# Householder tridiagonalisation on one NeuronCore: reciprocal of the divisor kept as the gain, a second ScalarE product, the minus-M form of the update, sign counts in blocks of eight, and the layers' loop written out

## The reference

```python
L_norm = d_inv_sqrt[:, None] * L * d_inv_sqrt[None, :]
_, U = jnp.linalg.eigh(L_norm)
agg = jnp.einsum('mn,bnd->bmd', U.T, features)
h = jax.nn.relu(agg @ W1 + b1)
out = h @ W2 + b2
return jnp.einsum('nm,bmd->bnd', U, out)
```

## Time and profile before

| | before |
|---|---|
| median of 3 runs | 1329.01 us |
| profiled execution | 1329.98 us, its span 1328.2 us |
| reflections, first to last tail written (L418) | 11.1 to 392.2 us |
| end of `spectral_basis` on VectorE (L441) | 402.67 us |
| start of the layers' first matmul | 523.44 us |
| VectorE, GpSimd busy in 0 to 403 us | 336.26, 286.13 us |
| granted TensorE clock in 0 to 403, 403 to 523, 523 to 1328 us | 1.00, 0.70, 0.94 |

### The profile page before, as it was taken

How to read it: one execution, slowest core, us unless ns; L and a number is a source line. 1 busy time by engine, 2 the same in 40 slices (tenths; PEclk the granted TensorE clock), 3 DMA queues, 4 the chain that set the end, 5 groups by cost and what they waited for, 6 DMA issues and landing times.

```text
span 1328.2 us, 24216 instructions
## 1 busy us (share of the span) xinstructions
PE 1079.3 (81%) x6225; PEld 889.4 (67%) x6225; DVE 987.5 (74%) x4609; ACT 807.5 (61%) x2954; POOL 401.2 (30%) x1534
## 2 busy tenths in 40 slices
PE   6888888777756773999787999787999787999785
PEld 5666666666654652689666689666689566689564
DVE  7888888888867996555779555778556779556777
ACT  4555555555542331577686677786677786677785
POOL 4777777777772000111111111111111101111201
PEclk9999999999999656999988999988999989999887
DMA  5000000000000242200000200000200000000001
GB/s 134 1 1 1 1 1 1 1 1 1 1 1 1 80 128 62 64 1 1 1 1 22 76 1 1 1 1 26 73 1 1 1 1 25 9 1 1 1 1 32
DMA packets 45239, 25.48 MB, mean 19 GB/s; under 512 B 1921, under 2 KB 44066, under 8 KB 45090
## 3 DMA queue, kind: packets, MB, share of 16 engines
q1 hardware_dynamic: 45090, 23.81, 6.5%
HBM read 15.42 MB, written 8.39 MB: 18 GB/s over the span
## 4 chain that ended last, share of the span: by engine, by line
PE 35%; DVE 12%; ACT 9%; issue 3%; POOL 1%; DVEq 0%; POOLq 0%; ACTq 0%
PE P L1205 12%; PE P L1153 6%; PE P L1213 6%; PE P L1158 2%; ACT x L1307 2%; ACT S L1375 2%; DVE stats L1414 2%; PE P L1267 2%; DVE S L1486 2%; DVE top L1491 1%; DVE t L1504 1%; PE P L1222 1%; PE P L1251 1%; POOL t L1141 1%; ACT t L1355 1%
## 5 line engine op out<-in xcount | busy, mean ns | idle before, releaser
L1134 POOL TENSOR_TENSOR rstd<-variance,minus_half 128x4 f32<-128x4 f32 x64 | 64.5, 1008 | 433.8 <-DVE variance L1424 433.8
L1205 PE MATMUL P<-t,WihT 128*128 128x128 f32 (+1 forms) x832 | 119.4, 290 | 11.0 <-POOL t L1141 11.0
L301 PE MATMUL tailP<-ident_tail 128*128 128x128 f32 (+63 forms) x254 | 87.7, 443 | 47.1 <-DVE ident_tail L418 46.0
L1213 PE MATMUL P<-step_h,WhhT 128*128 128x128 f32 (+2 forms) x768 | 123.4, 304 | 0.0
L1327 ACT ACTIVATE gate_i<-P,half_bias 128x128 f32<-128x128 f32 (+3 forms) x160 | 69.2, 433 | 89.0 <-PE P L1213 65.0
L1205 PEld LDWEIGHTS P<-t,WihT 128*128 128x128 f32 x832 | 109.9, 191 | 14.5 <-POOL t L1141 13.8
L1213 PEld LDWEIGHTS P<-step_h,WhhT 128*128 128x128 f32 x768 | 108.9, 191 | 4.5 <-DVE step_h L1457 0.7
L306 PE MATMUL productP<-M,ident_tail 128*128 128x127 f32 (+63 forms) x254 | 87.2, 440 | 30.1 <-DVE M L432 29.6
L301 PEld LDWEIGHTS tailP<-ident_tail 128*128 128x128 f32 x254 | 63.6, 311 | 71.2 <-DVE ident_tail L418 69.9
L1141 POOL COPY t<-HT 128x504 f32<-128x504 f32 (+1 forms) x32 | 31.9, 996 | 251.6 <-DVE HT L1457 234.8
L1375 ACT ACTIVATE S<-S,ntop 128x128 f32<-128x128 f32 x256 | 98.6, 390 | 0.0
(11 more groups left out here) (332 smaller groups left out, 3153.2 us busy)
## 6 DMA issues: line engine op xcount, KB each, us to landing
x_here<-x SPq DMA_DIRECT2D x16, 256.0 KB, 3.0
xin<-x SPq DMA_DIRECT2D x16, 256.0 KB, 3.1
feature_products<-made SPq DMA_DIRECT2D x16, 256.0 KB, 2.4
xw<-feature_products SPq DMA_DIRECT2D x16, 256.0 KB, 3.4
out<-y SPq DMA_DIRECT2D x16, 256.0 KB, 2.3
W<-L_gnn_W SPq DMA_DIRECT2D x3, 64.0 KB
Wqkv<-L_gnn_W SPq DMA_DIRECT2D x1, 192.0 KB
Wg<-L_gnn_Wg SPq DMA_DIRECT2D x2, 64.0 KB
```

The source lines that it names most:

```text
L301: pe.matmul(tailP[:, now:N + 1], tails, ident_tail[:, now:N + 1], start=True, stop=True).then_inc(tail_row_ready, 1)
L1134: nc.gpsimd.tensor_tensor(rstd[s][:], variance[s][:], minus_half[:], ALU.pow).then_inc(S_("rstd_ready"), 1)
L1205: last = pe.matmul(place, c["WihT"][:, p - 1, gate * H:(gate + 1) * H], sources(s, p, t), start=bank not in fresh, stop=not t, skip_group_ ...
L1213: last = pe.matmul(gate_place(s, p, t, gate), c["WhhT"][:, p - 1, gate * H:(gate + 1) * H], step_h[s][:, 0:G * windows(p)], start=False, s ...
```

## The change

In the reflections:

- The divisor becomes (|first| + norm) x norm, so its reciprocal is the gain (tau) itself. The pair of reciprocals (gain and 1/norm) is written straight into `gains[:, k, :]`, beta into `betas[:, k]`, the reflector into `reflectors[:, k]`. The copies to keep them, the two scaled gains ahead of L411 and the scaling by the norm go; one product, `KB` = gain x beta, is formed after L411.
- |first| is taken by ScalarE from PSUM (`sizes`) between L332 and L333.
- `open_gain` is made by ScalarE; ScalarE also multiplies the masked tail by 1/norm (`unit_tail`). GpSimd still masks the tail.
- The opened row is computed ahead of the reflector.
- The first update of M forms p x GV - M, the second v x NU - (that); the signs of the small terms are changed to fit.
- There are 126 reflections; VectorE finishes the last edge, the last two minors and the counts after them.

On GpSimd the difference of grid and diagonal is formed for a whole piece of the diagonal at once, minors of eight steps are kept, and their signs are counted together in three operations of 128 elements, one in each of three later steps. The squares of edges and the masking of the diagonal move ahead of the minors. In the last five reflections two minors are done in each.

In `spectral_vectors` one small VectorE operation is added on the way to the vectors' signs. In `layers` the loop is written out: same stages, constant waits and addresses.

```diff
-REFLECTIONS = N - 1
+REFLECTIONS = N - 2
...
-RESIZE = 8
 BATCH = 4
-CUTS = list(range(0, N - BATCH + 1, BATCH)) + [N - 2, N]
+SINGLE = N - 2 * BATCH
+CUTS = list(range(0, SINGLE + 1, BATCH)) + [N - 6, N - 4, N - 2, N]
+PIECES = len(CUTS) - 1
+CHUNK = 8
+WRITTEN = 2
...
+            def subtract_diagonal(b):
+
+                many = CUTS[b + 1] - CUTS[b]
+                pool.wait_ge(diag_kept, b + 1)
+                c.step(nc.gpsimd.tensor_tensor(apart[b % 2][:, 0:many, :], grid[:, None, :].to_broadcast([N, many, SHIFTS]),
+                                               D[:, CUTS[b]:CUTS[b + 1], None].to_broadcast([N, many, SHIFTS]), ALU.subtract))
...
+                c.done(nc.gpsimd.tensor_tensor(weighted[:], here, minor(m, chunk), ALU.mult))
+                c.step(nc.gpsimd.tensor_tensor(minor(m + 1, chunk), minor(m - 1, chunk), nE2[:, m - 1:m].to_broadcast([N, SHIFTS]),
+                                               ALU.mult))
+                c.step(nc.gpsimd.tensor_tensor(minor(m + 1, chunk), minor(m + 1, chunk), weighted[:], ALU.add))
...
+            def count_signs(chunk, part):
+                polynomials = minors[chunk % 2]
+                if part == 0:
+                    c.step(nc.gpsimd.tensor_tensor(agree[:], polynomials[:, 1:CHUNK + 1, :], polynomials[:, 2:CHUNK + 2, :], ALU.mult))
+                if part == 1:
+                    c.step(nc.gpsimd.tensor_scalar(agree[:], agree[:], 0.0, None, ALU.is_gt))
+                if part == 2:
+                    c.step(nc.gpsimd.tensor_tensor(votes[:], votes[:], agree[:], ALU.add))
...
             def minors_of_step(k):
                 lag = CUTS[1] + 1
-                if k < REFLECTIONS - 2:
+                fast = REFLECTIONS - 5
+                if k < fast:
                     return [k - lag] if k >= lag else []
-                first = REFLECTIONS - 2 - lag
-                return [first + 2 * (k - REFLECTIONS + 2), first + 2 * (k - REFLECTIONS + 2) + 1]
+                first = fast - lag + 2 * (k - fast)
+                return [m for m in (first, first + 1) if m < N - WRITTEN]
 
             def reflect(k, remaining, parity):
                 now = k + 1
                 pool.wait_ge(tail_ready, now)
                 nc.gpsimd.tensor_tensor(open_tail[:], tail, below[:, now:now + 1], ALU.mult).then_inc(open_tail_ready, 1)
+                if now in CUTS:
+                    take_diagonal(CUTS.index(now) - 1)
+                if k > SINGLE:
+                    square_edges(k - 1, k)
+                elif k in CUTS[1:]:
+                    square_edges(k - BATCH, k)
                 for m in minors_of_step(k):
                     next_minor(m)
-                pool.wait_ge(inverses_ready, now)
-                nc.gpsimd.tensor_tensor(open_gain[:], inverses[:, 1:2], below[:, now:now + 1],
-                                        ALU.mult).then_inc(open_gain_ready, 1)
-                if k in CUTS[1:]:
-                    square_edges(CUTS.index(k) - 1)
-                for m in minors_of_step(k):
-                    count_sign(m)
-                    if m < N - 8:
+                    if m < N - CHUNK:
                         keep_size(m)
-                if now in CUTS:
-                    take_diagonal(CUTS.index(now) - 1)
+                    if m >= CHUNK and m % CHUNK < 3:
+                        count_signs(m // CHUNK - 1, m % CHUNK)
 
             every_reflection(reflect)
...
                 if k in CUTS[1:]:
                     keep_diagonal(CUTS.index(k) - 1)
-
+                beta, gain, unit = betas[:, k:k + 1], gains[:, k, 0:1], gains[:, k, 1:2]
                 act.wait_ge(beta_ready, now)
+                act.wait_ge(inverses_ready, now)
+                nc.scalar.activation(open_gain[:], below[:, now:now + 1], ACT.Copy, scale=unit).then_inc(open_gain_ready, 1)
+                act.wait_ge(open_tail_ready, now)
+                nc.scalar.activation(unit_tail[:], open_tail[:], ACT.Copy, scale=unit).then_inc(unit_tail_ready, 1)
                 act.wait_ge(matrix_ready, now)
-                nc.scalar.activation(col(BETA_M), M[:, now:now + 1], ACT.Copy, scale=col(BETA)).then_inc(beta_m_ready, 1)
-                nc.scalar.activation(E[:, k:k + 1], col(BETA), ACT.Copy, scale=-1.0).then_inc(edges_ready, 1)
+                nc.scalar.activation(col(BETA_M), M[:, now:now + 1], ACT.Copy, scale=beta).then_inc(beta_m_ready, 1)
                 act.wait_ge(v_ready, now)
-                act.wait_ge(gain_ready, now)
-                nc.scalar.activation(col(NGV), v_col[:], ACT.Copy, scale=col(NTAU)).then_inc(scaled_ready, 1)
-                act.wait_ge(scaled_ready, now)
-                nc.scalar.activation(col(NGV_NORM), col(NGV), ACT.Copy, scale=norm).then_inc(scaled_norm_ready, 1)
-                nc.scalar.activation(reflectors[:, k:k + 1], v_col[:], ACT.Copy)
-                nc.scalar.activation(gains[:, k:k + 1], col(NTAU), ACT.Copy, scale=-1.0).then_inc(stored, 1)
+                nc.scalar.activation(col(GV), reflectors[:, k:k + 1], ACT.Copy, scale=gain).then_inc(scaled_ready, 1)
 
             every_reflection(reflect)
-            keep_diagonal(len(CUTS) - 2)
...
                 t.value = base_count + k * per
                 now = k + 1
                 after = k + 2
-                square, v_row = row_square[parity][:, N:N + 1], row_square[parity][:, remaining]
+                v_row = row_square[parity][:, remaining]
                 first = row_square[parity][:, now:now + 1]
+                beta, gain, reflector = betas[:, k:k + 1], gains[:, k, 0:1], reflectors[:, k:k + 1]
+                norm = divisors[parity][:, 1:2]
 
 
                 v.wait_ge(row_copied, now)
-                sign = signs[:, k:k + 1]
-                norm = divisors[parity][:, 1:2]
-                t.done(V.scalar_tensor_tensor(col(ABS), first, -1.0, first, ALU.mult, ALU.max))
-                prepared = t.done(V.tensor_scalar(sign, first, 0.0, 2.0, ALU.is_ge, ALU.mult))
+                signed = t.done(V.tensor_scalar(col(SIGN), first, 0.0, 2.0, ALU.is_ge, ALU.mult))
+                v.wait_ge(size_ready, now)
                 v.wait_ge(norm_ready, now)
-                t.until(prepared)
-                divided = t.done(V.scalar_tensor_tensor(divisors[parity][:, 0:1], col(ABS), norm, square, ALU.add, ALU.mult))
-                V.scalar_tensor_tensor(col(BETA), sign, 1.0, norm, ALU.subtract, ALU.mult).then_inc(beta_ready, 1)
+                divided = t.done(V.scalar_tensor_tensor(divisors[parity][:, 0:1], sizes[:, parity:parity + 1], norm, norm, ALU.add, ALU.mult))
+                t.until(signed)
+                V.scalar_tensor_tensor(beta, col(SIGN), 1.0, norm, ALU.subtract, ALU.mult).then_inc(beta_ready, 1)
                 t.until(divided)
-                V.reciprocal(inverses[:], divisors[parity][:]).then_inc(inverses_ready, 1)
+                V.reciprocal(gains[:, k, :], divisors[parity][:]).then_inc(inverses_ready, 1)
                 v.wait_ge(beta_ready, now)
-                V.scalar_tensor_tensor(v_col[:], ident[:, now:now + 1], col(BETA), tail, ALU.mult, ALU.add).then_inc(v_ready, 1)
-                whole_row = t.done(V.tensor_tensor(first, first, col(BETA), ALU.add))
+                opened = t.done(V.tensor_tensor(first, first, beta, ALU.add))
+                V.scalar_tensor_tensor(reflector, ident[:, now:now + 1], beta, tail, ALU.mult, ALU.add).then_inc(v_ready, 1)
                 v.wait_ge(inverses_ready, now)
-                V.scalar_tensor_tensor(col(NTAU), inverses[:, 0:1], -1.0, norm, ALU.mult, ALU.mult).then_inc(gain_ready, 1)
-                t.done(V.scalar_tensor_tensor(col(NKB), inverses[:, 0:1], -1.0, col(BETA), ALU.mult, ALU.mult))
-
-
                 v.wait_ge(product_ready, now)
-                t.until(whole_row)
-                t.done(V.tensor_tensor_reduce(out=scrap[:, remaining], in0=productP[:, remaining], in1=v_row, scale=inverses[:, 0:1], scalar=0.0,
+                t.until(opened)
+                t.done(V.tensor_tensor_reduce(out=scrap[:, remaining], in0=productP[:, remaining], in1=v_row, scale=gain, scalar=0.0,
                                               op0=ALU.mult, op1=ALU.add, accum_out=col(COEF)))
+                t.done(V.scalar_tensor_tensor(col(KB), gain, 1.0, beta, ALU.mult, ALU.mult))
                 v.wait_ge(product_col_ready, now)
                 v.wait_ge(open_gain_ready, now)
                 t.step(V.scalar_tensor_tensor(col(Q), product_colP[:, 0:1], open_gain[:], spark[:, after:after + 1],
                                               ALU.mult, ALU.subtract))
-                v.wait_ge(open_tail_ready, now)
-                V.scalar_tensor_tensor(tail, open_tail[:], col(COEF), col(Q), ALU.mult, ALU.subtract).then_inc(tail_ready, 1)
-
-
-                v.wait_ge(gain_ready, now)
+                v.wait_ge(unit_tail_ready, now)
+                V.scalar_tensor_tensor(tail, unit_tail[:], col(COEF), col(Q), ALU.mult, ALU.subtract).then_inc(tail_ready, 1)
+
+
```

(39 more changed lines are left out.)

## The result

The changed kernel takes 1283.8 us (median of 4 runs, 1282.94 to 1286.47) against 1328.33 us for the kernel before on the same chip (4 runs, 1323.90 to 1329.28): a ratio of 0.9675, 95% interval 0.9648 to 0.9701. The profiled execution took 1283.95 us, its span is 1282.1 us. The forecast was 1283.4. It came out to half a microsecond, but three of its terms were off by 4 to 8 us, in both directions. That they cancelled so well is luck. The rest of this text is about those.

A forecast was written before the change was run, and what follows sets the result against it. The 380 us of reflections were taken as one serial chain, VectorE having hardly a gap. Terms of -17.7 (GpSimd), -14.4 (chain), -10.5 (end), -3.5 (loop) and +0.5 (small) summed to -45.6: 1283.4 us against the median, range 1271 to 1299.

The forecast's parts named there:

- the likeliest case: Whole kernel: all terms come as summed, 1283.4 us, with an own range of 1278 to 1290; chance 0.50.
- item 1: Reflections: with open_gain on ScalarE, VectorE's stalls for GpSimd go, gain 17.7 us, bounds 12.9 and 23.2.
- Rival B: Middle reflections: GpSimd still holds VectorE up through the masked tail, 24 waits of 0.33 us, 8 us, 1291; chance 0.10.
- item 2: VectorE's chain of one reflection: 0.12 us shorter on average, 14.4 us for 120 reflections, bounds 0 and 24.
- T: Start of the divisor in each reflection: 0.51 to 0.57 us behind the row's copy instead of 0.59.
- rival A: Reflections: the chain gives nothing back, VectorE's removed distance becomes waiting for ScalarE or L311, 1298 us; chance 0.20.
- item 3: From the tail of reflection 120 to VectorE's end: 20.5 us instead of 31.0, gain 10.5, bounds 7 and 13.
- item 4: Layers' loop written out: trips of 198.87 and 197.64 us fall to 196.48, gain 3.5 us, bounds 0 and 6.
- Rival D: Reflections: Abs makes ScalarE reload tables twice each, 2.56 x 126 = 323 us, 1606 us; chance 0.03.
- 2.68 at 64 columns: Sign in the profile after: time in us from one reflection's tail to the next, at 64 columns.
- Sixteen stalls of 0.3 to 0.4: Sign in the reflections' profile after: stalls of 0.3 to 0.4 us without a late engine stay some 16 in number.
- The end near 361: Sign in the profile after: the last VectorE operation of spectral_basis comes near 361 us.

## Why the prediction was right in sum and wrong in its terms

**What bounds, and the account's form: right.** The reflections are one chain on VectorE, GpSimd's gain was the periodic disturbance, and half of the gain lies there. The forecast range and the likeliest case held.

**GpSimd off the path (item 1): -17.7 forecast, -13.8 measured.** The wait that I read from the earlier trace rows did go: moving the gain alone brought 13.1 us. But 17.7 was a remainder, all stalls less 5.5, and not what the waits add up to: the 12.9 us that I had as the lower bound were nearer to both 13.1 and 13.8. In the changed kernel the step that failed is the one that counted GpSimd's work as free once nobody waits for it. I had listed its load (0.9 to 2.7 us a reflection) and compared it with the period, and never asked what a GpSimd operation of 128 elements does to the VectorE operation that runs beside it. It costs 4.8 us over 120 reflections, by the run without counting. The waits' view can't show this: no engine waits, an operation merely takes 0.38 instead of 0.15. All other disturbances came to 4.2 us in that run, against 5.5 forecast; so without the counting the term would have come out, with the two errors in it (fewer such stalls, less waiting for GpSimd) against each other. Rival B (waits for the masked tail in the middle) didn't happen.

**The chain (item 2): -14.4 forecast, -9.0 measured.** T came as forecast (0.54 behind the row's copy). The term that was mis-sized is the start of the projection, put at T + 0.60 from an interval of 0.54 to 0.62: it was 0.65 to 0.69, 0.04 to 0.05 behind the end of the reflector operation beside it (193.65 + 0.21 to 193.91) and 0.32 behind the start of the opened row's (193.59). That is 0.05 to 0.09 us a reflection. Two limits fall together there. The one is the order on VectorE: where a GpSimd operation delays L414, the projection follows L414's end (at k = 61, shown above, it starts 0.06 ahead of the stretched operation's end). The other is the semaphore of the opened row, which alone gives 0.33 us in the run with the reflector first. So T + 0.66 couldn't have been beaten by shortening either alone. The trace of before had the first already, in a row that I hadn't shown: L406, 0.15 us long, starts at 203.52, and L411 at 203.68, right behind its end, while L405 and L406 themselves start 0.07 behind one another. I took the overlap of small operations as possible for this one too. I had also let the product with M end 0.08 us ahead of its reader; the shortest such distance in any reflection is 0.13, so that cover wasn't there, which in the 27 reflections where it binds costs 0.3 us in all. With it, 0.12 becomes 0.06 to 0.08, and 9.0 / 120 is 0.075. The signs of rival A, waits for L311 or for ScalarE, are absent in the middle. That the matrix would be late next was right: KB moved away from the tail's path brought its wait at once.

**The end (item 3): -10.5 forecast, -11.3 measured**, in 19.7 us against 20.5, with the masked tails of the last reflections late as forecast. The gain on ScalarE is worth 6.9 us there (from tail 120 to the last tail 21.7 us without it, 14.9 with it), against 1.8 in the 120 reflections ahead.

**The loop (item 4): -3.5 forecast, -11.6 measured with the last trip.** The failed step is "taking the last as the price of a straight trip": the trip of 196.48 us had 20.6 us at the lower clock, and a straight trip with 10.1 us takes 194.3. I took one execution's trip for a constant. The two turns are worth some 3.4 to 6.5 us by the comparison at the same clock; my own 3.5 is at the lower edge of that. The Trainium skill's rule (Runtime: NRT & Kernel Launch, section Instruction fetch mechanics), of a fetch at each taken branch outside the fetched window, gave 5.9, which lies inside. The remainder is clock. Of it the 3.1 us of the last trip came in every execution, the rest moves from one execution to the next: by medians the written-out loop alone is worth 7.4 us, by the profiled spans 10.0, and the latter is what the account above is made of.

**Rival D, table reloads:** there is none among the reflections; L344 takes 0.17 us. The Trainium skill (ScalarE: Activation LUTs, section Table sets: the hidden batching unit) says that abs is in every set; the trace agrees, with L344, L343 and L345 back to back (190.07, 189.95, 190.12).

**What I said the profile would show:** no wait of Q for GpSimd and no "issue" of 2.95 us at the trips, right. 2.68 at 64 columns: 2.71 to 2.77. Near 2.9 wide and 2.46 narrow: 2.93 to 3.0 and 2.56 to 2.58, so the gain shrank most at the narrow end. Sixteen stalls of 0.3 to 0.4: half as many, two in 32 reflections and some 0.25 us long, and the two waits of 8 times are down to one of 4. The end near 361: 368.8. Trips all near 196.5: 195.9, 194.2, 194.4. Read at the time, these would have shown the sum to be right for partly wrong reasons.

## What to carry to other kernels

Work moved off the critical engine isn't free because nobody waits for it: compare the lengths of the critical engine's small operations with and without the neighbour's wide ones, since the view of waits is blind to it. In a chain of dependent small operations, put independent ones into the gap between a producer and a reader that needs its semaphore; here that order alone was worth 12.8 us of the change. And before taking a stage's time from one execution, look at the granted clock in it: here the same program's trips through the layers differed by 5 us between two executions, more than some of the gains ahead of them.

## What the runs showed of the hardware that I had not expected

- A GpSimd operation on two tensors of 128 x 128 (0.45 us) stretches a VectorE operation of one column with two inputs in SBUF beside it, from 0.15 to 0.38, or 0.21 to 0.42 us; one with a single tensor operand (0.54 us) doesn't. In pieces of 64 elements (0.32 us) the loss over 120 reflections is 1.7 to 2.0 instead of 4.8 us (335.24 and 334.95 against 333.25).
- The multiply with a reduction starts 0.04 to 0.05 us after the VectorE operation ahead of it is shown to end in most reflections of the changed kernel, at that end (0.00 to 0.01) in most of before, where plain small operations start 0.07 to 0.08 before it.
- Leaving a hardware loop cost nothing that could be seen, turning back in it some 3.4 to 6.5 us for two turns. The straight code behind the loop ran 3.1 us longer (185.03 against 181.90 in the windows above), with TensorE at its lower clock for 25.8 instead of 14.9 us of the first 176; what ties that to the loop is open.
